# Row factor of the graph-attention layers on ScalarE, key blocks added on VectorE ahead of the denominators, and new orders, in a four-layer graph kernel

## The reference: what is computed

```
g[j] * max(T[i], c[j]) * mask[i, j]
```

## Time and profile before

| | |
|---|---|
| median of three runs | 4387.51 us (4381.95 to 4387.93) |
| the profiled execution's own time | 4386.9 us |
| its span, first to last instruction | 4385.0 us |
| mean granted TensorE clock | 0.975 of full speed |
| PE busy | 4098.6 us, 93% |
| DVE busy | 3228.5 us, 74% |
| ACT busy | 2161.6 us, 49% |

### The profile page before, as it was taken

How to read it: one execution, slowest core, us unless ns; L and a number is a source line. 1 busy time by engine, 2 the same in 40 slices (tenths; PEclk the granted TensorE clock), 3 DMA queues, 4 the chain that set the end, 5 groups by cost and what they waited for, 6 DMA issues and landing times.

```text
span 4385.0 us, 59504 instructions
## 1 busy us (share of the span) xinstructions
PE 4098.6 (93%) x22822; PEld 1952.0 (45%) x22884; DVE 3228.5 (74%) x6985; ACT 2161.6 (49%) x3361; POOL 334.5 (8%) x469
## 2 busy tenths in 40 slices
PE   4799999999999999999999999999999999999997
PEld 1344444444444444444444444444444444444443
DVE  5577777877777877777877777877777877778754
ACT  3344455544455544455544455444455444455432
POOL 0000000000000000000001000000000000001000
PEclk9899999999999999999999999999999999999998
DMA  2111101122202112201122201122111122111100
GB/s 87 29 44 54 54 20 54 34 54 54 54 20 54 34 54 54 54 20 49 39 54 54 49 25 49 39 54 54 46 28 49 39 54 54 38 36 48 26 30 29
DMA packets 212314, 193.92 MB, mean 44 GB/s; under 512 B 144448, under 2 KB 179008, under 8 KB 203584
## 3 DMA queue, kind: packets, MB, share of 16 engines
q1 hardware_dynamic: 212032, 190.12, 16.4%
HBM read 138.95 MB, written 17.56 MB: 36 GB/s over the span
## 4 chain that ended last, share of the span: by engine, by line
PE 60%; DVE 23%; ACT 9%; issue 4%; DMA 2%; SPq 1%; POOL 0%; POOLq 0%; ACTq 0%; DVEq 0%
PE M L435 10%; DVE PG L1017 7%; PE O L474 6%; PE M L422 6%; PE M L446 6%; PE M L488 5%; PE S L521 5%; DVE x L934 4%; DVE PP L903 4%; PE S L355 3%; PE O L537 3%; PE O L478 3%; ACT PP L622 3%; PE M L579 3%; PE M L413 2%
## 5 line engine op out<-in xcount | busy, mean ns | idle before, releaser
L622 ACT ACTIVATE PP<-S,reach 128x1024 f32<-128x1024 f32 x512 | 542.4, 1110 | 375.1 <-PE S L355 249.0
L1017 DVE SCALAR_TENSOR_TENSOR PG<-g,tcg,mT 128x512 f32<-128x512 f32 x1024 | 692.4, 740 | 12.8 <-DMA g<-t_rows 10.8
L903 DVE TENSOR_TENSOR PP<-PP,mT 128x1024 f32<-128x1024 f32 x512 | 598.6, 1215 | 75.4 <-ACT PP L622 75.4
L474 PE MATMUL O<-PG,V 128*32 128x512 f32 x4096 | 565.1, 646 | 15.3 <-DVE PG L1017 14.6
L647 ACT ACTIVATE z<-x,nb,rs 128x256 f32<-128x256 f32 x384 | 206.6, 596 | 556.6 <-DVE nb L893 556.4
L422 PE MATMUL M<-hT,W 128*128 128x512 f32 x1024 | 460.6, 603 | 2.8 <-ACT hT L657 2.0
L435 PE MATMUL M<-W,H 128*128 128x256 f32 x2048 | 463.0, 380 | 0.0
L435 PEld LDWEIGHTS M<-W,H 128*128 128x128 f32 x2048 | 379.7, 190 | 62.6 <-issue 0.3
L1046 DVE TENSOR_TENSOR PP<-PP,m 128x1024 f32<-128x1024 f32 x256 | 301.5, 1219 | 87.1 <-ACT PP L736 87.1
L1128 POOL TENSOR_SCALAR ve<-mv 128x4 f32<-128x4 f32 x192 | 80.9, 421 | 3456.5 <-DVE mv L861 3109.0
L355 PE MATMUL S<-hT 32*128 32x512 f32 x2048 | 295.0, 645 | 28.7 <-ACT PP L622 27.8
(11 more groups left out here) (136 smaller groups left out, 5367.7 us busy)
## 6 DMA issues: line engine op xcount, KB each, us to landing
g<-t_rows SPq DMA_DIRECT2D x64, 1024.0 KB, 5.7
adj<-adj_in SPq DMA_DIRECT2D x32, 1024.0 KB, 6.0
x<-x_in SPq DMA_DIRECT2D x32, 512.0 KB, 6.8
z<-t_rows SPq DMA_DIRECT2D x64, 256.0 KB, 4.0
out<-x SPq DMA_DIRECT2D x32, 512.0 KB, 7.2
W<-w_in SPq DMA_DIRECT2D x1, 3072.0 KB, 16.4
mT<-z SPq DMA_TRANSPOSE x128, 4.4
m<-V SPq DMA_TRANSPOSE x128, 5.4
```

Of the source, the lines that this page charges most:

```text
L474: e.matmul(k.O[0][r:r + 32, :], s.V[:, jt, 64 * hh + 32 * v:64 * hh + 32 * v + 32], p[:, u, :], start=(jt == 0), stop=(jt == NT - 1))
L622: e.activation(p[:, 2 * pair:2 * pair + 2, :], k.S[:, 2 * pair:2 * pair + 2, :], ACT.Exp, bias=k.reach[:, 7:8], scale=SC0).then_inc(k.e0.s ...
L903: e.tensor_tensor(p[:, 2 * pair:2 * pair + 2, :], p[:, 2 * pair:2 * pair + 2, :], s.mT[:, jt:jt + 1, :].to_broadcast([128, 2, N]), ALU.mul ...
L1017: e.scalar_tensor_tensor(out=p[:, u, :], in0=s.T[hh], scalar=s.tcg[:, 1, hh, jt:jt + 1], in1=s.mT[:, jt, :], op0=ALU.max, op1=ALU.mult).th ...
```

## The change

Four things change together.

1. ACT gets a step `gw`: 16 activations for each layer and batch, Copy of a bf16 mask block 128x512 with g[j] as a scale for each partition, into `PG`. DVE's `gw` then multiplies by `PG` in place instead of by the mask, and waits for each of these.
2. `gvals` and the tile `Gp` go away, with the two activations that filled it.
3. DVE gets a step `pag`, four times for each layer and batch: one TENSOR_TENSOR 128x1024 that adds two key blocks into `Q`. PE's 16 denominator matmuls for each layer and batch become 8, in a step `dng` that runs twice.
4. The orders are new. The semaphores of the row transfers of layers 1 and 2 are shared.

```diff
 class Act
+    def gw(self, b, L, c):
+        pr, jp = c // 2, c % 2
+        p = k.PG[jp]
+        self.take(f"PG{jp}", k.gpv[L].at(b, c))
+        self.take(f"PG{jp} added", k.qg[L].at(b, c))
+        self.wait_ge(*k.gtc[L].at(b, 0))
+        self.wait_ge(*k.lm[0].at(b))
+        for u in range(4):
+            jt, hh = 2 * jp + u // 2, 2 * pr + u % 2
+            e.activation(p[:, u, :], s.mT[:, jt, :], ACT.Copy, scale=s.tcg[:, 2, hh, jt:jt + 1]).then_inc(k.gmk[L].sem, 1)
 class Dve
     def gw(self, b, L, c):
-        self.take(f"PG{jp}", k.gpv[L].at(b, c))
-        self.wait_ge(*k.gtc[L].at(b, 0))
-        self.wait_ge(*k.lm[0].at(b))
-        self.wait_ge(*k.lt[L].at(b))
+        self.wait_ge(*k.lt.nth(b, L - 1))
         for u in range(4):
-            e.scalar_tensor_tensor(out=p[:, u, :], in0=s.T[hh], scalar=s.tcg[:, 1, hh, jt:jt + 1], in1=s.mT[:, jt, :],
+            self.wait_ge(*k.gmk[L].at(b, 4 * c + u))
+            e.scalar_tensor_tensor(out=p[:, u, :], in0=s.T[hh], scalar=s.tcg[:, 1, hh, jt:jt + 1], in1=p[:, u, :],
                                    op0=ALU.max, op1=ALU.mult).then_inc(k.gm[L].sem, 1)
+    def pag(self, b, L, c):
+        if jp == 0:
+            self.take("Q", k.dng[L].at(b, pr))
+        self.wait_ge(*k.gm[L].at(b, 4 * c + 3))
+        e.tensor_tensor(k.Q[:, 2 * jp:2 * jp + 2, :], p[:, 0:2, :], p[:, 2:4, :], ALU.add).then_inc(k.qg[L].sem, 1)
-    def gvals(self, b, L):
...
 class Pe
     def gpv(self, b, L, c):
-        for u in range(4):
-            m = e.matmul(k.O[1][32 * u:32 * u + 32, :], k.Gp[b % 2][:, jt, hh, :], p[:, u, :], start=(c == 0), stop=(c == 3))
+    def dng(self, b, L, pr):
+        if pr == 0:
+            self.take("O1", k.god[L].at(b, 0))
+        for u in range(4):
+            self.wait_ge(*k.qg[L].at(b, 2 * pr + u // 2))
+            m = e.matmul(k.O[1][32 * u:32 * u + 32, :], k.unit[:, pr, :], k.Q[:, u, :], start=(pr == 0), stop=(pr == 1))
+        m.then_inc(k.dng[L].sem, 1)
 class Act
     def gprep(self, b, L):
-        for pr in range(2):
-            i = e.activation(k.Gp[b % 2][:, :, 2 * pr:2 * pr + 2, pr].rearrange("p t h -> p h t"),
-                             s.ex[:, 2, 2 * pr:2 * pr + 2, :], ACT.Exp)
     def gout(self, b, L, pr):
         if pr:
+            self.wait_ge(*k.dng[L].at(b, 1))
             e.copy(s.DT, k.O[1][:, :]).then_inc(k.god[L].sem, 1)
```

More of the change, by code:

```diff
@@ L300, in gpv, with pag, dng @@
     def gpv(self, b, L, c): pass
+    def pag(self, b, L, c): pass
+    def dng(self, b, L, pr): pass
     def gout(self, b, L, pr): pass
@@ L1319, in tensor_program @@
         do.gpv(b2, 1, 2)
+        do.dng(b2, 1, 0)
         do.sc0(b1, 1)
@@ new lines, in tensor_program @@
+        do.sc3(b3, 3)
+        do.dn3(b3, 0)
+        do.prep_b(b1)
+        do.tt(b1, 0, 0)
+        do.tt(b1, 0, 1)
+        do.pv3(b3, 2)
+        do.w1(b1, 0)
+        do.pv3(b3, 3)
+        do.w1(b1, 1)
+        do.w1(b1, 2)
+        do.w1(b1, 3)
+        do.grow(b2, 2)
+        do.dn3(b3, 1)
+        do.w1(b1, 4)
+        do.w1(b1, 5)
+        do.den3(b3)
+def scalar_program(do):
+    for it in range(1, NB + 3):
+        b1, b2, b3 = it - 1, it - 2, it - 3
+        do.w1(b2, 7)
+        do.gw(b3, 2, 0)
+        do.gw(b3, 2, 1)
@@ L1532, in vector_program @@
+        do.pag(b3, 2, 2)
+        do.pag(b3, 2, 3)
         do.wo(b4, 1)
-        do.gw(b3, 2, 3)
         do.bag(b1, 1, 3)
-        do.gvals(b2, 1)
         do.rc(b3, 2, 0)
@@ new lines, in vector_program @@
+        do.bst(b2, 4, 0)
+        do.rc(b2, 1, 3)
+        do.b2r(b2, 1, 2)
+        do.b2r(b2, 1, 3)
+        do.sc0(b1, 3)
+        do.pa0(b1, 1)
+        do.bag(b2, 4, 0)
+        do.bst(b0, 0, 0)
+        do.bst(b2, 4, 1)
+        do.bag(b2, 4, 1)
+        do.sc0(b1, 4)
+        do.bst(b2, 4, 2)
+        do.bag(b2, 4, 2)
+        do.bst(b2, 4, 3)
+        do.bag(b2, 4, 3)
+        do.sc0(b1, 5)
+        do.nb(b2, 4)
+        do.pa0(b1, 2)
+        do.masks(b0, 0)
+        do.bst(b0, 0, 1)
+        do.sq3(b3, 0)
@@ new lines, in vector_program @@
+        do.sc0(b1, 6)
+        do.bst(b0, 0, 2)
+        do.sc0(b1, 7)
+        do.pa0(b1, 3)
+        do.sq3(b3, 1)
+        do.zb(b1)
+        do.sh3(b3)
+        do.rc(b1, 0, 0)
+        do.bst(b0, 0, 3)
+        do.bag(b0, 0, 0)
+        do.bag(b0, 0, 1)
+        do.b2r(b1, 0, 0)
+        do.fin(b1, 0, 0)
+        do.rc(b1, 0, 1)
+        do.b2r(b1, 0, 1)
+        do.rc(b1, 0, 2)
+        do.b2r(b1, 0, 2)
+        do.sc3(b3, 0)
+        do.bst(b1, 2, 0)
+        do.rc(b1, 0, 3)
+        do.pa3(b3, 0)
@@ new lines, in vector_program @@
+        do.b2r(b1, 0, 3)
+        do.bag(b0, 0, 2)
+        do.fin(b1, 0, 1)
+        do.bst(b1, 2, 1)
+        do.fin(b1, 0, 2)
+        do.pj(b2, 2, 0)
+        do.fin(b1, 0, 3)
+        do.bag(b1, 2, 0)
+        do.bst(b1, 2, 2)
+        do.bag(b0, 0, 3)
+        do.bst(b1, 2, 3)
+        do.bag(b1, 2, 1)
+        do.bag(b1, 2, 2)
+        do.bag(b1, 2, 3)
+        do.sc3(b3, 1)
+        do.pj(b2, 2, 1)
+        do.resid0(b1)
+        do.nb(b1, 2)
+        do.prep_b(b1)
+        do.prep_w(b1)
@@ new lines, in vector_program @@
+        do.pa3(b3, 1)
+        do.pj(b2, 2, 2)
+        do.sc3(b3, 2)
+        do.pj(b2, 2, 3)
+        do.pa3(b3, 2)
+        do.gmax(b2, 2)
+        do.sc3(b3, 3)
+        do.pa3(b3, 3)
+        do.gprep(b2, 2)
+        do.den3(b3)
+        do.masks(b0, 1)
+        do.w2(b1, 0)
+def gpsimd_program(do):
+    for it in range(0, NB + 3):
+        b0, b1, b2, b3 = it, it - 1, it - 2, it - 3
+        do.rs(b2, 3)
+        do.gmax(b2, 1)
+        do.rs(b1, 1)
+        do.rs(b3, 5)
+        do.rs(b2, 4)
+        do.rs(b1, 2)
+        do.gmax(b2, 2)
+        do.rs(b0, 0)
```

479 lines of the change are left out of this document (191 added, 288 removed).

## The result

The changed kernel takes 4531.86 us (median of 4 runs, 4529.6 to 4532.24) where the kernel before takes 4387.72 us beside it (4381.95 to 4390.03). The ratio is 1.0328, with a 95% interval of 1.0315 to 1.0340: the change makes the kernel 3.3% slower.

A forecast was written before the change was run, and what follows sets the result against it. It took DVE's work in stretch A plus PE's in stretch B to bound each pass: 70.8 + 1.0, handovers 0.3, B 63.1, or 135.2 us against 132.1. 4386.9 + 90 - 10 = 4467 us, range 4355 to 4545.

The forecast's parts named there:

- stretch A: Pass from DVE's first rc of layer 2 to layer 3's second sc3: DVE work 59.4 + 11.4 = 70.8 us.
- Stretch B: Pass from layer 3's pv3 to the transposes rc needs: 66.96 - 4.6 + 0.7 = 63.1 us, PE work 59.8.
- DVE's total: DVE busy time over the whole execution: near 3445 us, rising from 100.9 to 107.6 us a batch.
- DVE's idle time in A: DVE's waits in stretch A, 3.6 us before, should shrink with PE waiting; 1.0 us taken, bounds 0 and 3.6.
- the ends: Filling before 361 us and draining after 4193 us: -10 us taken, between -30 and +20.
- One loop over all of A: A pass cannot be shorter than DVE's work in stretch A plus PE's in B; summed to 135.2 us.
- PE's total: PE busy time over the whole execution: near 3980 us, with 118 us of denominator matmuls gone.
- PE everywhere: Rival: PE bounds the whole pass, 3.7 us come off each and DVE's additions hide; 4269 us, chance 0.10.
- the milder form: Milder first rival: the summed loop with no idle time, 130.9 us a pass or 4342 us; chance 0.07.
- the two cancel: Rival: idle time shrinks so far that the pass stays at 132 us, about 4387 us; chance 0.08.
- ACT late: Rival: DVE's 16 gw in stretch A each wait 0.12 us for ACT, +1.9 us a pass, 4522 us; chance 0.06.
- The rival of the clock: Rival: PE at the lower clock for most of stretch A, +5 us a pass, 4612 us; chance 0.07.

The follow-up runs named there:

- masks_to_b: The changed kernel with DVE's masks(b0,0) moved from stretch A to just ahead of den3 in stretch B; 4541.47 us, ratio 1.032 to the kernel before.
- old_orders_new_math: Kernel before's orders in stretch A, layer 2's steps in new places in stretch B, new arithmetic in both layers; 4537.16 us, ratio 1.0346 to the kernel before.
- pag_a_out: The changed kernel without layer 1's four pag, its dng reading a constant tile; 4455.23 us, ratio 1.0124 to the kernel before.

## Why the prediction was right, and where it wasn't

**The sign and the place: right.** The loss is in stretch A, the gain in B, and they were sized well. Stretch B was to take 63.1 us and takes 63.14; DVE's work in A was to be 70.8 us and is 70.53. B's total hides two errors that cancel: PE's work in it was to be 59.8 us and is 61.08, and the waits, 3.3 us by the prediction (66.96 - 64.41 + 0.7), are 2.1. DVE's total was to be near 3445 us and is 3450.2, ACT's near 2800 and is 2777.7, though the prediction's own 90 us a batch would make 2870: an instruction of `gw` adds 0.64 us in a row of four, not 0.69. `gw` on DVE kept its duration (744 ns), and ACT is ahead. DVE's waits for `den3` and `w2` come to 22 us a batch, (372.4 + 324.4) / 32, where some 20 were forecast.

**The sum: 4467 predicted, 4531.9 measured.** The pass is 136.7 us and not 135.2. B agrees in its total; A measures 73.70 us from its start to its end where 70.8 + 1.0 plus the handovers were summed. So the mis-sized term is DVE's idle time in A: 1.0 us taken, within bounds of 0 and 3.6, and 73.70 - 70.53 = 3.17 us measured in this pass. With 0.3 us less work of DVE and 0.3 us less between the stretches this is the 1.6 us by which this pass is longer than forecast, 1.5 us in the mean, or 43 us in all. The other term is the ends: -10 us taken, and 2.2 + 10.5 = +13 measured, 23 us. Together they are the 65 us between prediction and result, but for rounding.

**Why the idle time did not shrink.** The step said that with PE waiting for DVE the late exponentials would come in time. In part they do. Before, DVE waited for three of them in the run of the pass shown, 1.05, 0.72 and 1.52 us. After, it waits for four, 1.46 us together, and for two transpositions of layer 0, 1.05 us together (columns in order of time):

```profile
2087.39 2.36 DVE L919 TENSOR_TENSOR PP<-PP,mT 128x1024 f32<-128x1024 f32 x2 [0.75 <-ACT PP L630]
2108.07 0.21 DVE L940 RECIPROCAL ri<-M 128x8 f32<-128x8 f32 x1 [0.82 <-PE M L400]
```

The prediction had named both kinds of wait but left them in a sum of 1.0. All of them stand in PE's run. The three windows show why: DVE is never idle in the front (0.05 us) and is idle for 2.9 us in PE's run, where PE binds, partly at the lower clock. One loop over all of A, as the prediction had it, is therefore not what binds. masks_to_b shows it from one side (DVE work taken out behind the handover brings nothing) and old_orders_new_math from the other (+4.7 us with 5.5 us of DVE's time in A idle). How much work could be added behind the handover for nothing was not tried. That the sum came close is partly luck: in this kernel the front of DVE plus the run of PE is nearly as long as DVE's work in A.

**The terms by cause.** The prediction charged A with 11.4 us, 4.5 of them for the additions and the rest for steps moved in by the orders. Six of the kernels, the two of the comparison among them, form a table of orders and arithmetic, mean A + mean B in us:

| | old arithmetic | layer 2 new | both new |
|---|---|---|---|
| old orders | 65.6 + 66.5 = 132.1 | 66.9 + 65.5 = 132.4 | 71.6 + 65.5 = 137.1 |
| new orders | 71.1 + 63.8 = 134.9 | 70.5 + 62.7 = 133.2 | 74.0 + 62.7 = 136.7 |

Read along the rows, layer 1's new arithmetic costs 4.7 or 3.5 us a pass, and layer 2's costs 0.3 or gains 1.7. Read down the columns, the new orders cost 2.8, 0.8 and -0.4 us. The two changes do not simply add. With the old arithmetic the orders cost 5.5 us in A and give 2.7 back in B. With the full arithmetic they cost 2.4 in A (74.0 for 71.6, with 4.5 us more work of DVE) and give 2.8 back in B, so there they are not at fault. Why they cost more alone was not separated. What holds in either order is the price of layer 1's new arithmetic, 4.7 or 3.5 us where the whole loss is 4.6. In the new orders most of it (2.5 of 3.5 us) is paid in the front: the additions, of which pag_a_out gave back 2.4 us a pass, and the chain of PE, ACT and DVE around them.

**PE's total: wrong.** Near 3980 us was forecast and 4115.0 measured, although the matmuls went: the denominators of layers 1 and 2 fell from 299.2 (L478) to 169.9 us (L486), 129 for the 118 forecast. In A PE is busy 66.03 us where 61 was forecast. Part is the granted clock: 0.93 over 73.70 us against 0.97 over 62.94 us is 5.2 - 1.9 = 3.3 us of full-speed time more that A loses. Other matmuls, unchanged in number, took longer, `gpv`'s by 37 us in all (L474 565.1, L475 602.1) and `pv0`'s by 23 (277.1 to 300.2). Some 14 us of the total are only records missing from the trace before (L509 25.4 us with 66 records, L517 39.4 with 128). The rest was not separated.

**The rivals.** PE everywhere (4269 us) falls, since DVE has no pause in the front and PE 7.4 us of them, and the milder form with it, since DVE is idle for 3.17 us in A. That the two cancel (4387 us) is refuted by the time. ACT late falls with 3.2 us of waits for it in the whole execution. The rival of the clock had the mechanism, but 5 us of it in place of the 0.9 us by which the run got longer. The Trainium skill (TensorE: Matmul & The Clock Gate, What's actually happening) has the lower clock as the default, released by activity; the rows agree in kind, with 0.88 in the front, where PE waits for 7.4 us, and 1.00 in B.

## What to carry to other kernels

Two in-order engines that wait for each other don't share one bound over a stretch: cut the pass at every last wait and ask which engine is without a pause in each piece. Work added ahead of a handover can be paid in full even where both engines show idle time around it (4.7 us for 4.7 in the old orders, 3.5 for 4.6 in the new ones), and work taken out behind it can bring nothing (masks_to_b). Work taken out ahead of it is returned only until the next chain binds: 2.4 us for 4.3 in pag_a_out. A change that applies one rewrite at two places should be timed at each place alone: here, in the new orders, the same rewrite gains 1.7 us a pass in one layer and loses 3.5 us in the other.
